# A fused two-layer block: first maxima and the token route spread over head groups, row loads on two queues

## What is computed

```python
xn = layernorm(x)
q, k, v = rope(xn @ wq), rope(xn @ wk), xn @ wv      # 32 query heads, 8 key heads
s = softmax(q @ k.T / 4 + causal_mask) @ v @ wo
_, top = top_k(xn @ W_gate + b_gate, 2)              # per token
y = relu(xn @ W_e[e] + b_e[e]) for e in top, mean of the two
x = x + s * silu(y)
xn = layernorm(x)
s = causal_convolution(xn, K) + D * xn               # K from the S4 parameters, over the channel axis
g = silu(xn @ dequant(weight).T + bias)
out = x + s * g
```

## Time and profile before

| | before |
|---|---|
| median of 3 runs | 762.63 us (761.85 to 764.82) |
| profiled execution | 762.54 us, span 760.8 us |
| mean granted TensorE clock | 0.917 of 2.4 GHz |
| PE busy | 681.8 us (90%), 3653 instructions |
| DVE busy | 531.4 us (70%) |
| ACT busy | 303.0 us (40%) |
| POOL busy | 251.9 us (33%) |

### The profile page before, as it was taken

How to read it: one execution, slowest core, us unless ns; L and a number is a source line. 1 busy time by engine, 2 the same in 40 slices (tenths; PEclk the granted TensorE clock), 3 DMA queues, 4 the chain that set the end, 5 groups by cost and what they waited for, 6 DMA issues and landing times. The chain is left out here.

```text
span 760.8 us, 12565 instructions
## 1 busy us (share of the span) xinstructions
PE 681.8 (90%) x3653; PEld 377.5 (50%) x3679; DVE 531.4 (70%) x1775; ACT 303.0 (40%) x553; POOL 251.9 (33%) x419
## 2 busy tenths in 40 slices
PE   3999956749999999999999999999999978869997
PEld 2888843334444443444443444444444433358886
DVE  4799878877757666676665776657766573359994
ACT  4344313323435443355433444344443432235442
POOL 2765521352232322222231222322222214446630
PEclk9999975558999999999999999999998997879999
DMA  7487877851726425154362432624415218648851
GB/s 228 145 271 266 266 185 175 218 91 31 132 71 120 89 60 105 42 95 87 62 132 59 78 75 47 123 75 98 80 41 96 67 45 279 135 79 191 207 137 69
DMA packets 52813, 92.25 MB, mean 121 GB/s; under 512 B 7800, under 2 KB 20664, under 8 KB 52752
## 3 DMA queue, kind: packets, MB, share of 16 engines
q1 hardware_dynamic: 40800, 64.21, 35.5%
q0 software_dynamic: 6704, 18.62, 10.9%
q10 hardware_dynamic: 5248, 8.69, 3.6%
HBM read 61.53 MB, written 29.43 MB: 120 GB/s over the span
## 5 line engine op out<-in xcount | busy, mean ns | idle before, releaser
L1179 DVE CUSTOM_DVE_ANT_0 bank<-bank,cst 128x384 f32<-128x384 f32 (+3 forms) x512 | 236.3, 518 | 142.2 <-PE bank L1358 140.0
L1283 ACT ACTIVATE arena<-bank 128x512 f32<-128x512 f32 x320 | 176.3, 602 | 126.8 <-PE bank L1380 85.1
L1103 POOL TENSOR_SCALAR_AFFINE_SELECT arena<-arena 128x512 f32<-128x512 f32 x128 | 81.6, 637 | 360.7 <-ACT arena L1283 360.6
L1437 PE MATMUL bank<-w_e,arena 128*128 x312 | 158.0, 617 | 4.6 <-issue 2.6
L1358 PE MATMUL bank<-kt,qt 48*128 48x384 f32 (+3 forms) x512 | 136.6, 370 | 13.2 <-DVE arena L1179 11.4
L1358 PEld LDWEIGHTS bank<-kt,qt 48*128 48x128 f32 x512 | 82.2, 208 | 113.0 <-DVE arena L1179 84.3
L1407 PE MATMUL bank<-arena 128*32 128x512 f32 (+3 forms) x1024 | 103.1, 502 | 0.0
L1380 PE MATMUL bank<-qt,kt 50*128 50x512 f32 x192 | 81.2, 525 | 14.2 <-DMA qt<-arena 10.5
L1437 PEld LDWEIGHTS bank<-w_e,arena 128*128 128x128 f32 x312 | 51.9, 190 | 55.2 <-issue 54.1
L1179 DVE DVE_READ_ACCUMULATOR2_ANT arena<- 128x1 f32 x512 | 71.9, 140 | 0.0
L1296 ACT ACTIVATE arena<-bank 128x512 f32<-128x512 f32 x39 | 23.3, 597 | 114.1 <-PE bank L1437 114.1
(11 more groups left out here) (162 smaller groups left out, 983.1 us busy)
## 6 DMA issues: line engine op xcount, KB each, us to landing
qt<-turned_parts SPq DMA_DIRECT2D x96, 128.0 KB, 4.9
turned_parts<-qk_parts SPq DMA_DIRECT2D x8, 1280.0 KB, 6.9
expert_rows<-arena SPq DMA_DIRECT2D x39, 256.0 KB, 2.0
w_e<-in_L_ffn_W_e ACTq DMA_DIRECT2D x8, 1024.0 KB, 7.2
kt<-turned_parts SPq DMA_DIRECT2D x96, 64.0 KB, 4.8
arena<-in_L_attn_x SPq DMA_DIRECT2D x16, 256.0 KB, 4.4
xn_rows<-arena SPq DMA_DIRECT2D x16, 256.0 KB, 2.8
w_e<-in_L_attn_x SPq DMA_DIRECT2D x16, 256.0 KB, 3.7
```

Of the source, the lines that this page charges most:

```text
L1103: g.affine_select(out=diag, in_=diag, compare_op=ALU.is_ge, fill=0.0, base=0, pattern=[[0, 2], [0, HALF], [1, P]], channel_multiplier=-1). ...
L1179: i = v.tensor_tensor_reduce(out=part, in0=part, in1=const("mask")[:, S - w:], scale=1.0, scalar=LOWEST, op0=ALU.add, op1=ALU.max, accum_o ...
L1283: a.activation(pt[:, s, 2 * i:2 * i + 2].rearrange("p c r q -> p (c r q)"), bank[2 + s], ACT.Exp, scale=HD ** -0.5)\
L1437: i = t.matmul(bank[7], xgt[:, k, :], w_e[:, ex[b * MPB + m], k, :], start=False, stop=(k == KB - 1))
```

## The change

It touches the order of stage b in six places.

- In stage a's tail all ten maxima of the first group come at once, then their parts, turn and copy; the turns and low parts of blocks 2 and 3 follow.
- The token route: `pe_route` moves into group 0 after burst 0; ScalarE copies its result after exps 1; POOL does the running sums (`running_counts` after select 0, `positions` after select 1, `chosen_slots` after select 3); VectorE keeps one comparison and reduction after maxima 5 of group 0. dve_route(0) and (1) stay at the ends of groups 0 and 1; `pe_back` moves into group 2 after burst 1, `dve_tokens` after maxima 5 of group 2, the first two gathers after select 2 of it.
- FIRST: tile 0 moves from group 2 to 3, and groups 3 to 7 have two tiles each.
- PAIRED: (2, 2) and (2, 3), which share their keys, make one matmul; (1, 3) and (3, 3) are the last pair. The exponentials write two blocks with a stride.
- `finish` of group h moves from between the next group's maxima to the end of group h, behind maxima_rows and dve_s4, which change places. On TensorE values 1 to 3 all follow the turn, and filler 1 precedes it.
- `maximum_rows` issues one DMA on SP's queue and one on ScalarE's; the second tile's copy (`expert_x`) moves up to step n = 7.

```diff
--- before.py
+++ after.py
+PAIRED = [((0, 0), (0, 1)), ((0, 2), (0, 3)), ((1, 1), (1, 2)), ((2, 2), (2, 3)), ((1, 3), (3, 3))]
@@ -496,18 +498,15 @@ dve_a
             turned_low(NB - 1, 1)
-            for n in range(4):
-                maxima(e, 0, 0, n)
-            turned_low(NB - 1, 2)
-            for n in range(4, 8):
-                maxima(e, 0, 0, n)
-            turned_low(NB - 1, 3)
-            for n in range(8, NJ):
+            for n in range(NJ):
                 maxima(e, 0, 0, n)
             maxima_parts(e, st, 0, 0)
-            for piece in range(TPB):
+            ranks(NB - 1, 0)
+            maxima_rows(e, 0, 0)
+            turned_low(NB - 1, 2)
+            for piece in range(1, TPB):
                 ranks(NB - 1, piece)
-            maxima_rows(e, 0, 0)
+            turned_low(NB - 1, 3)
@@ -856,8 +855,9 @@ pe_a
-                if n in (2, 6):
-                    turn_qk(NB - 1, 2 + n // 4)
+            turn_maxima(e, 0, 0)
+            for u in (2, 3):
+                turn_qk(NB - 1, u)
@@ -868,41 +868,16 @@ dve_route (the running sums and products leave it)
             if h < 0:
-                e.wait_ge(r_count, 1)
...
+                e.wait_ge(r_scan, 1)
+                cmp = compared[:, 0:E * NT].rearrange("p (e i) -> p e i", e=E)
+                tt(cmp, scan_b[:, NT - 1, :].unsqueeze(2).to_broadcast([P, E, NT]), const("i128").unsqueeze(1).to_broadcast([P, E, NT]), ALU.is_gt)
+                v.tensor_reduce(end_b, cmp, AX.X, ALU.add).then_inc(r_ceil, 1)
+            if h == 0:
+                e.wait_ge(r_flat, 2)
+                for k, pick in enumerate((first, second)):
+                    v.tensor_reduce(slot_f[:, k, :], pick, AX.X, ALU.add).then_inc(dve_steps, st.one())
...
@@ -945,6 +919,7 @@ pe_route
+            e.wait_ge(a_ql, NT)
             e.wait_ge(r_chosen, NB)
@@ -1031,7 +1006,7 @@
-        FIRST = [(None, None), (None, None), (0, None), (1, 2), (3, 4), (5, 6), (7, None), (8, 9)]
+        FIRST = [(None, None), (None, None), (None, None), (0, 1), (2, 3), (4, 5), (6, 7), (8, 9)]
@@ -1094,14 +1068,61 @@ pool_b
+            def running(a, spare, last, n):
+                step = 1
+                while step < n:
+                    o = last if 2 * step >= n else spare
+                    g.tensor_copy(o[:, 0:step], a[:, 0:step]).then_inc(r_steps, 1)
+                    taken()
+                    tt(o[:, step:], a[:, step:], a[:, 0:n - step], ALU.add)
+                    a, spare, step = o, a, 2 * step
+
+            def running_counts():
+                e.wait_ge(r_copied, 1)
+                alone(e)
+                tt(pos, pos, tot, ALU.subtract)
+                running(tot, scan_a, scan_b, NT)
+                tt(pos, pos, scan_b, ALU.add)
+                e.nop().then_inc(r_scan, 1)
+
+            def positions():
+                e.wait_ge(r_ceil, 1)
+                alone(e)
+                g.tensor_copy(tiles_of, end_b).then_inc(r_steps, 1)
+                taken()
+                running(end_b, scan_a[:, 0, :], end_a, E)
+                tt(end_b, end_a, tiles_of, ALU.subtract)
+                g.tensor_scalar(end_b, end_b, float(P), None, ALU.mult).then_inc(r_steps, 1)
+                taken()
+                tt(pos, pos, end_b.unsqueeze(1).to_broadcast([P, NT, E]), ALU.add)
+
+            def chosen_slots():
+                g.tensor_tensor(first, first, pos, ALU.mult).then_inc(r_flat, 1)
+                g.tensor_tensor(second, second, pos, ALU.mult).then_inc(r_flat, 1)
@@ -1138,16 +1159,23 @@ pool_b, go
-                    select(b, h)
+                    for j in range(TPB):
+                        select(b, h, j)
+                        if not due(b) and h == 0 and j == 0:
+                            running_counts()
+                        if not due(b) and h == 0 and j == 1:
+                            positions()
+                        if not due(b) and h == 2 and j == 2:
+                            for u in range(TPB):
+                                e.wait_ge(a_store[u], 16 * NB)
+                            e.wait_ge(r_tokens, 1)
+                            gather(0, 0)
+                            gather(0, 1)
+                    if not due(b) and h == 0:
+                        chosen_slots()
...
-                    if not due(b) and h == 1:
-                        for u in range(TPB):
-                            e.wait_ge(a_store[u], 16 * NB)
-                        e.wait_ge(r_tokens, 1)
-                        gather(0, 0)
-                        gather(0, 1)
@@ -1228,63 +1256,48 @@ dve_b
+            def finish(b, h):
+                rows_of(b, h)
+                normalise(b, h)
+                if h % 2 and (due(b) or h > 1):
                     pair_rows(b, h // 2)
@@ dve_b, go
                             maxima(e, *next_group(b, h, 1), n)
-                        finish(b, h - 1, n)
+                        if not due(b) and h == 0 and n == 5:
+                            dve_route(e, st, -1)
+                        if not due(b) and h == 2 and n == 5:
+                            dve_tokens(e, st)
+                            pair_rows(0, 0)
                     if h + 1 < NG or more:
                         maxima_parts(e, st, *next_group(b, h, 1))
-                    dve_s4(e, st, b, h)
                     if h + 1 < NG or more:
                         maxima_rows(e, *next_group(b, h, 1))
+                    dve_s4(e, st, b, h)
+                    finish(b, h)
                     if not due(b) and h < 2:
                         dve_route(e, st, h)
-                    if not due(b) and h == 1:
-                        dve_tokens(e, st)
...
-            dve_route(e, st, -1)
@@ -1303,12 +1326,18 @@ act_b, go
+                        if not due(b) and h == 0 and n == 1:
+                            e.wait_ge(r_count, 1)
+                            a.copy(pos.rearrange("p t e -> p (t e)"), bank[7][:, 0:P])
+                            a.copy(tot.rearrange("p t e -> p (t e)"), bank[7][:, P:2 * P]).then_inc(r_copied, 1)
...
-                    if second is not None:
-                        expert_x(b, second)
+                        if n == Y_AT and second is not None:
+                            expert_x(b, second)
+                    if h + 1 < NG or more:
+                        maximum_rows(e, *next_group(b, h, 1), 1)
@@ -1369,7 +1397,7 @@ scores_2
-            pair = BLOCKS[2 * i:2 * i + 2]
+            pair = PAIRED[i]
@@ -1478,50 +1506,29 @@ pe_b, go
+                        if burst == 0 and not due(b) and h == 0:
+                            pe_route(e)
+                        if burst == 1 and not due(b) and h == 2:
+                            pe_back(e)
...
-                    if second is not None:
-                        expert(b, h, second, 0)
-                    values(b, h, 1)
+                            if second is not None:
+                                expert(b, h, second, 0)
                     filler(0)
+                    filler(1)
                     if following:
-                        turn_maxima(*following)
-                    values(b, h, 2)
-                    values(b, h, 3)
-                    for k in range(1, 4):
-                        filler(k)
-
-            turn_maxima(0, 0)
-            e.wait_ge(a_ql, NT)
-            pe_route(e)
+                        turn_maxima(e, *following)
+                    for j in range(1, TPB):
+                        values(b, h, j)
+                    filler(2)
+                    filler(3)
@@ -1521,7 +1550,7 @@ sp_b
-                        maximum_rows(e, *next_group(b, h, 1))
+                        maximum_rows(e, *next_group(b, h, 1), 0)
```

More of the change, by code:

```diff
@@ L326, in build @@
         r_tokens = sem("r_tokens")
+        r_copied, r_steps, r_scan, r_ceil, r_flat = (sem(n) for n in ("r_copied", "r_steps", "r_scan", "r_ceil", "r_flat"))
         block = ctx.enter_context(nc.Block())
@@ L901, in dve_route @@
-            if h == 0:
-                for k, pick in enumerate((first, second)):
-                    tt(pick, pick, pos, ALU.mult)
-                    v.tensor_reduce(slot_f[:, k, :], pick, AX.X, ALU.add).then_inc(dve_steps, st.one())
-                    e.wait_ge(dve_steps, st.count())
+            if h < 0:
+                e.wait_ge(r_scan, 1)
+                cmp = compared[:, 0:E * NT].rearrange("p (e i) -> p e i", e=E)
+                tt(cmp, scan_b[:, NT - 1, :].unsqueeze(2).to_broadcast([P, E, NT]), const("i128").unsqueeze(1).to_broadcast([P, E, NT]), ALU.is_gt)
+                v.tensor_reduce(end_b, cmp, AX.X, ALU.add).then_inc(r_ceil, 1)
@@ new lines, in taken, with tt @@
+            def taken():
+                steps[0] += 1
+                e.wait_ge(r_steps, steps[0])
+            def tt(out, a, b, op):
+                g.tensor_tensor(out, a, b, op).then_inc(r_steps, 1)
+                taken()
[7 more added lines that the diff above has]
+                    a, spare, step = o, a, 2 * step
```

(7 more changed lines are left out.)

80 lines of the change are left out of this document (22 added, 58 removed).

## The result

The changed kernel takes 773.34 us (766.04 to 779.73) beside 763.24 (758.94 to 767.56) for the kernel before on the same chips: a ratio of 1.011, 95% interval 1.009 to 1.014. It is slower by 1.1%, where 742.5 (731 to 755) was forecast. The profiled execution has a span of 768.4 us (760.8 before) and a mean granted clock of 0.911 (0.917).

The account below looks back on a forecast made before the run. TensorE bounds from 259.7 to 623.1 us, a VectorE chain from 100.1 to 181.3, a last-group chain after 623.1. Span 760.8 - 3.2 - 10.0 - 5.7 - 1.2 + 0 = 740.7, plus 1.7 is 742.4, by the median 742.5 (731 to 755).

Parts of the forecast that it names:

- Up to group 3: Groups 0 to 2: group 2's maxima start at 135.9, dve_route(1) at 149.8, group 3 at 174.2 instead of 181.20.
- POOL beside VectorE: Token route in group 0: POOL takes 0.47 us per 128x128 step, 4.3 us for running_counts, 3.0 for positions.
- rival 3: Token route: VectorE slows POOL and the kernel gets slower, 774 us at 1.5 us a step; chance 0.05.
- up to the turn for batch 1: First maxima and token route moved: group 7 ends at 256.5 instead of 259.7, -3.2 us.
- five late groups: Groups with a tile wholly in the fillers (h = 4 and 6): 13.0 us each, 75.0 in all before, -10.0 us.
- twelve with a projection: Projection groups: waits for m-rows and expert_x go, 15.55 us each, 192.3 in all before, -5.7 us.
- six with two tiles: Groups with two tiles in batches 1 to 3: 15.8 us each, 96.0 in all before, -1.2 us.
- behind the last turn: After the last group's maxima: projection still starts at about 649.3, 0 us (-3.5 to +1.5).
- the sentence on the row copy and the two DMAs in the third part: Group ends: row copy ahead of dve_s4, m-row DMAs side by side instead of 0.63 apart; within projection groups' -5.7 us.
- Rival 4: Gathers and loads that come later eat the gains: within 0.5%, 760 us; chance 0.06.
- Late groups of 13 us without a fall of the clock: Sign of success: groups with a tile wholly in the fillers shorten from 14.57 to 13.0 us, refuted if still 14.6.
- The end: Last scores to projection: scores start at 623.2, taps wait 2.5 us for dft, projection still at about 649.3, 0 us.

Follow-up runs that it names:

- SP's wait: Changed kernel, nothing moved: SP waits until both m-row DMAs have landed before issuing an odd group's stack loads; 740.7 us, ratio 0.972.
- the kernels with moved or narrowed loads: Changed kernel with stack loads behind the even group's fourth scores (750.4 us) or second (747.0 us), or cut to a thirty-second of the bytes (746.2 us).
- that kernel: Changed kernel with SP waiting for both m-row DMAs before odd groups' stack loads, and both m-row DMAs on SP's queue again; 758.3 us, ratio 0.990.

## Why the prediction was wrong

**Up to group 3: right.** VectorE waits for POOL once, 1.06 us (forecast 1.5); the maxima of group 2 start at 135.64 (135.9), dve_route(1) at 149.97 (149.8), group 3's first scores at 172.19 (174.2, where 181.20 stood). From there to the turn for batch 1 it took 86.9 us, where it was 74.8 before and 80.3 with SP's wait.

```profile
122.17 0.29 DVE L868 TENSOR_TENSOR arena<-arena,cst 128x128 f32<-128x128 f32 x1 [1.06 <-POOLq L1106]
...
135.64 0.70 DVE L1207 CUSTOM_DVE_ANT_0 bank<-bank,cst 128x512 f32<-128x512 f32 x1
...
149.97 4.41 DVE L894 TENSOR_TENSOR arena<-arena,iota_b 128x4096 bf16<-128x4096 bf16 x1
```

**POOL beside VectorE: right, and rival 3 didn't occur.** In group 0 the 128x128 steps took 0.45 us beside VectorE's maxima (0.47 assumed); beside the large VectorE instruction at 149.97 a select of 0.64 us took 4.36:

```profile
118.11 0.45 POOL L1086 TENSOR_TENSOR arena<-arena 128x128 f32<-128x128 f32 x1
```

```profile
150.51 4.36 POOL L1076 TENSOR_SCALAR_AFFINE_SELECT arena<-arena 128x512 f32<-128x512 f32 x1 [0.75 <-ACT arena L1306]
```

The Trainium skill (SBUF — State Buffer, "Who interferes with whom") says that a VectorE instruction with two SBUF inputs contends with a GpSimd instruction that reads SBUF, and that one with at most one SBUF input, outside the two-port modes, does not. Both rows agree: the instruction at 149.97 has two inputs in SBUF, the maxima have one in PSUM and one in SBUF.

**The sum: right once the loads are away.** The forecast's terms beside both kernels, by turns (us, against the kernel before):

| term | forecast | changed | with SP's wait |
|---|---|---|---|
| up to the turn for batch 1 | -3.2 | +3.0 | -2.9 |
| five late groups (75.0) | -10.0 | +2.7 | -11.2 |
| twelve with a projection (192.3) | -5.7 | +2.6 | -4.0 |
| six with two tiles (96.0) | -1.2 | -1.7 | -2.5 |
| behind the last turn | 0 | +1.0 | -1.1 |
| span, sum | -20.1 | +7.6 | -21.6 |

In the column with SP's wait the terms are rounded each by itself. The kernel of that column was not the one forecast; it shows that the terms were sound once the loads are held back. Its good agreement is in part luck: the kernels with moved or narrowed loads, just as free of the contention, came to 746 to 750 us, 3 to 8 us of it by their late groups.

**The step that failed** is the sentence on the row copy and the two DMAs in the third part. It counted what an earlier m-row gains and stopped there. Behind the m-rows on SP's queue stand the twelve stack loads of every odd group, and they were moved forward too; the turn moved as well, so the gather no longer went out first. That step was priced as a gain, and a later gather at nothing. Undone singly, neither the copy's order (774.3) nor the second queue (775.9) gave anything back, and the turn's order with the pairs gave 14 us; what costs is that all of them bring the loads up to the gather and the m-rows. It cost, by the one wait that undoes it, 773.3 - 740.7 = 32.6 us, and by the three other ways of keeping the loads' bytes away 23 to 27. The 29.2 us between the spans fall on the late groups (13.9), the twelve with a projection (6.6), the time up to batch 1 (6.0), the end (2.1) and the six with two tiles (0.7). Over batches 1 to 3 these are 21.2 us by the traces (366.9 and 345.7), of which the waits for gathers and m-rows make 11.3 (14.6 and 3.3); most of the rest is TensorE at its lower level (mean clock 0.95 beside 0.99, busy time 350.4 beside 337.0 us). Rival 4 named gathers and loads, with the sign turned round (loads that come later), held it to the size of the gain and gave it 0.06. Rival 3, the one on the slow side, looked at POOL; the price came from DMA.

**"Late groups of 13 us without a fall of the clock"** was a second slip inside a right mechanism: at full clock and without a stop they take 12.1, with a stop of 1.19 us 13.7, and where the clock falls to 0.8 or less 15 or more (14.2 and 14.4 at 0.88 in two other kernels). One size was not to be had. The mean with SP's wait, 12.8, is four groups of 12.1 to 12.2 and one of 15.3, so that the term's size came out right by luck; the falls in the earlier trace rows at 229 us (0.88) were read as the result of VectorE's waits alone.

**The end: right by size (+1.0 for 0), for partly other reasons.** The wait of 4.05 us went, and the taps waited 4.14 us instead of 2.5; by the times it was for dft, whose DMA was issued at 630.55 and took 9.4 us. Then the projection waited 5.81 for VectorE:

```profile
640.01 6.19 PE L649 MATMUL bank<-w_e,roots 128*128 128x512 f32 x8 [4.14 <-issue]
...
657.07 3.78 PE L1479 MATMUL bank<-w_proj,arena 128*128 128x512 f32 x4 [5.81 <-DVE arena L630]
```

## What to carry over

When a small transfer is moved forward, list what stands behind it on its queue: it moves too, and if it is large it may now run beside something urgent. A bulk load with slack can be made to wait for the urgent transfers' landing (one wait on the issuing queue), which returned 4.2% here and cost the kernel before nothing that can be measured (0.998). In a stage where TensorE is full, price a stall by its length plus the stretch at the lower clock that may follow.

## What the runs showed of the hardware

- An indirect gather of a tile landed mostly in 3.3 to 3.8 us with no loads beside it. It took 4.0 to 5.9 us when twelve loads of 64 and 128 KB began 0.83 us behind it on another queue, and 5.4 to 8.5 when it was issued 1.1 to 1.3 us behind the first of them; with a thirty-second of their bytes it took 3.4 to 4.4.
- Waits of 0.2 to 0.5 us ahead of scores_2 went along with 3 us more in four of five late groups, by the clock (12.1 us at 1.00, 15.2 at 0.78). Over batches 1 to 3 that kernel has 15 such waits (4.9 us) and the one beside it four (1.0 us); they differ by 17.6 us.
